# Half of the first mixture's source tiles moved into attention's tail, and VectorE's small tiles of routing in a PSUM bank of its own

## The chip, the cores and the metric

The kernel runs on one core of one Trainium2 chip. The metric is the device time of one execution in microseconds (us), the median of several. Engines: PE is TensorE, DVE is VectorE, ACT is ScalarE, POOL is GpSimd, SP is the engine that issues the DMAs here.

## The reference

Four layers with a residual each, on x of shape (2, 1024, 128), all in float32. The change touches the first two and the routing of the fourth.

```
x = x + attn_a(layernorm(x))     # 16 heads of 64, keys serve as values, causal, out @ W_out (1024 x 128)
x = x + ffn(layernorm(x))        # mixture of experts, with its own inner residual
x = x + attn_b(layernorm(x))     # gated state-space layer with a convolution of 3 taps
x = x + ffn(layernorm(x))

def ffn(x):
    logits = sigmoid(x @ gate_w + gate_b)                  # 16 experts
    values, idx = top_k(logits, k=2); values /= values.sum()
    y_e = (silu(x @ wg_e) * (x @ wu_e)) @ wd_e             # for each expert, inner width 64
    return x + shared_mlp(x) + sum over the two chosen of values * y_e
```

## The kernel before

The 2048 tokens are 16 tiles of 128, or 4 groups of 512 (four tiles each: `PER` is 4, `GROUPS` is 4). x lies in SBUF as `k.x`. The program is a sequence of blocks; inside a block each engine has its own instruction list, and a block's border is passed by all engines together, when the last has finished. Attention is a block, the first mixture (`m1`) the next, then the state-space layer, then the second mixture (`m2`).

**Attention** works in 16 units, each a pair of heads for one of the two batches; unit 14 and 15 are the last pair. A unit's products with the keys, `outputs(g, r)`, come in five bursts, one unit behind the scores. Burst 0 makes the first half of the queries, bursts 1 to 4 the second, in the same PSUM bank `out_ps`, so burst 1 waits until `scale_out(g, 0)` on DVE has read it. POOL adds up the exponentials in `sums`, which lies in the room of `k.x` (its first half of query columns is groups 0 and 2 of x, its second half groups 1 and 3). `denominators(g, half)` (L694 for the last unit) sum these over partitions, ACT inverts them. The scores use three pairs of PSUM banks in turn (`ring_uses`). In the loop's last round, with unit 16, only `outputs(15, r)` and the second denominators are left on TensorE. SP loads W_out (`load_w_out`) at the end of its list.

**A mixture** goes over 36 steps (nine per group: two experts each, the ninth the shared one). A step on TensorE is six matmuls into `g` and `u` and the `down` matmuls of two steps before; ACT makes silu of g, POOL multiplies it with the expert's weight per token (`m_prod`, L1134; the weights come by a DMA into `wb`), DVE multiplies by u (`m_hid`, L1043). The matmuls into `u` wait for hid of two steps before. Everything else is a piece with a time of its own, counted in steps of the group: `agenda` sorts the pieces by `PREPARE`, `OWN`, `FINISH` and `SOURCE_TILES`, and each engine issues its own pieces in that order between the steps. Pieces with a time under 0 come ahead of step 0; of pieces with equal time the order is that of `ORDER`. The pieces are:

- source: eight matmuls per tile of attention's output with W_out (L1715), into the banks of g and u; DVE adds the result to x (L1051)
- statistics, root (ACT, a Sqrt with its own table), norm (DVE: reciprocal L801, then four instructions in `scale_rows`, L96), turn (four transposes, L823), high and low: the split of the normed x into two parts
- residual (POOL, L1143), logits (L963 to L965), sigmoid, natural (transposes back), route1 to route3 (top 2, indices, shares, w: L1077 to L1098), turn_w and w_high; SP then stores w (L1176) and spreads it into wb (L1154)
- add_up and, in m1, the norm for the next layer (`after`), in the finish of a group

In m1 SP first issues the four loads of x, then the eight weight transfers (L1161 to L1169), then the state-space weights (`ahead_of.load`), and only then does its list come to w. ACT waits for all eight transfers ahead of gate_hi (L1005), wg_hi and wu_hi; DVE makes gate_lo (L1070) behind gate_hi, and the logits of group 0 wait for it (`low_split`). `scale_taps` on POOL comes ahead of the residual of group 3, `split_high` and `split_low` of the state-space weights behind the root and the norm of the finish of group 1. A `GroupNorm` named `first` already serves m2: there group 0's source, statistics and root lie in the state-space block.

Of the kernel before, what the change touches and what calls it, by code (L numbers as in the profile page):

```python
# [20 lines left out]
ALU = mybir.AluOpType  # L21
# [78 lines left out]
def layernorm_transposed(nc, s, k, load, banks, xn, sync_first, vector_first, gpsimd_work):  # L100
# [36 lines left out]
    with nc.Block() as block:  # L137
        @block.sync
        def _(sp):
            load(sp, x_loaded)  # L140
            sync_first(sp)
# [82 lines left out]
def ring_uses():  # L224
# [12 lines left out]
    return uses  # L237


def attention(nc, k, w_qk, load_x, load_w_out):  # L240
# [3 lines left out]
    with Scope(nc, "at") as s:  # L244
# [32 lines left out]
        den_ready, ln_done, inv_done, out_used = s.sem("den_ready"), s.sem("ln_done"), s.sem("inv_done"), s.sem("out_used")  # L277
        inv_spread = [s.sem(f"inv_spread{h}") for h in range(2)]
# [90 lines left out]
        with nc.Block() as block:  # L369
            @block.sync  # L370
            def _(sp):
# [21 lines left out]
                load_w_out(sp)  # L393

# [120 lines left out]
            def _(dve):  # L515
# [75 lines left out]
                for half in range(2):  # L591
                    scale_out(UNITS - 1, half)

            @block.tensor
            def _(pe):
# [105 lines left out]

                project(0, "K")
# [48 lines left out]
               low=-12, logits=-10, sigmoid=-9, natural=-8, route1=-8, route2=-8, route3=-7, turn_w=-5, w_high=-5)  # L751
# [8 lines left out]
OWN = {0: dict(norm=-16, residual=-15, turn=-14, high=-13, low=-13, route2=-7, route3=-6),  # L760
# [24 lines left out]
class GroupNorm:  # L785


    def __init__(self, s, tag):
        self.xn = s.sb(f"{tag}_xn", [P, PER, D])
        self.stats, self.moments = s.sb(f"{tag}_stats", [P, PER, 6]), s.sb(f"{tag}_moments", [P, PER, 2])  # L790
        self.sd, self.rstd = [s.sb(f"{tag}_{n}", [P, PER]) for n in ("sd", "rstd")]
        self.small, self.varied, self.rooted, self.normed, self.turned, self.high, self.low = [
# [6 lines left out]
    def norm(self, dve, n, x):  # L799
        dve.wait_ge(self.rooted, n + 1)  # L800
        dve.reciprocal(self.rstd[:, :], self.sd[:, :]).then_inc(self.small, 1)  # L801
# [25 lines left out]
def mixture(nc, tag, k, f, source, source_ready=None, load_x=None, weights=None, next_norm=False, store=None, ahead_of=None, first=None):  # L827
# [9 lines left out]
    with Scope(nc, tag) as s:  # L837
# [10 lines left out]
        x_loaded = [s.sem(f"x_loaded{n}") for n in range(GROUPS if load_x else 0)]  # L848
        sourced, added, summed = s.sem("sourced"), s.sem("added"), s.sem("summed")
        before, after = first or GroupNorm(s, "before"), GroupNorm(s, "after") if next_norm else None  # L850
        early = 1 if first else 0
# [5 lines left out]
        at_f, share = s.sb("at_f", [P, 2, PER]), s.sb("share", [P, 2, PER])  # L857
        picked, parts = s.sb("picked", [P, 2, PER, EXPERTS]), s.sb("parts", [P, 2, PER, EXPERTS])
        den, rec = s.sb("den", [P, PER]), s.sb("rec", [P, PER])
# [17 lines left out]
        def interleave(pieces, emit, step, tiles=False):  # L877

            todo = [item for item in agenda(pieces, next_norm, tiles)
                    if item[2] >= early or item[1] not in ("source", "statistics", "root")]  # L880
# [11 lines left out]
        with nc.Block() as block:  # L892
            @block.tensor
            def _(pe):
# [44 lines left out]
                def emit(piece, n, kind):  # L939
                    if piece == "source":  # L940
                        if source_ready and n == 0 and kind == 0:
                            source_ready(pe)
# [40 lines left out]
            def _(act):  # L983
# [7 lines left out]
                def emit(piece, n, kind):  # L991
                    norm = before if kind == "prepare" else after
                    if piece == "root":
                        norm.root(act, n, k.eps)
                        if ahead_of and n == 1 and norm is after:
                            ahead_of.split_high(act)
# [18 lines left out]
                    elif piece == "w_high":  # L1015
                        act.wait_ge(wt_ready, n + 1)
                        wait(act, wt_stored, 16 * n)
                        act.activation(f.wt[:, :], misc[1][0:EXPERTS, :], ACT.Copy).then_inc(wt_done, 1)
                interleave(("root", "high", "sigmoid", "w_high"), emit, step)

            @block.vector
            def _(dve):
# [22 lines left out]
                def emit(piece, n, kind):  # L1045
                    norm = before if kind == "prepare" else after
                    if piece == "source":
                        dve.wait_ge(sourced, n + 1 - early)
                        if load_x:
                            dve.wait_ge(x_loaded[n], 16)  # L1050
# [3 lines left out]
                    elif piece == "statistics":  # L1054
                        if norm is before:
                            dve.wait_ge(added, n + 1 - early)
# [3 lines left out]
                    elif piece == "norm":  # L1060
# [3 lines left out]
                        if ahead_of and n == 1 and norm is after:  # L1064
                            ahead_of.split_low(dve)
# [684 lines left out]
```

## Time and profile before

| what | value |
|---|---|
| median of 3 runs | 784.04 us (783.72 to 785.32) |
| the profiled execution | 783.28 us |
| its span | 781.5 us |
| PE busy | 729.7 us (93%) |
| DVE / ACT / POOL busy | 458.5 / 375.6 / 424.4 us |
| mean granted clock of TensorE | 0.989 |
| m1's block opens | 492.3 us |
| first step of m1 | 523.44 us |

A busy PE is not a PE at its peak, but an idle PE does nothing: the table and the stretches say where it waits. Idle time of another engine counts only where PE waits for it.

### The profile page before, as it was taken

How to read it: one execution, taken by the hardware profiler on the slowest of the kernel's cores; microseconds unless marked ns; L12 is line 12 of the kernel's file. 1: busy time of each engine (PE TensorE's matmuls, PEld its weight loads, DVE VectorE, ACT ScalarE, POOL GpSimd, SP SyncE). 2: the span in 40 equal slices, each digit the busy share in tenths (PEclk: the TensorE clock that was granted, in tenths of full speed). 3: DMA queues.
4: the chain of work that ended last, by engine and by line, in shares of the span. 5: the costliest groups of instructions: out<-in, count | busy, mean ns of one | idle time of the engine just before them, and what ended most of it. 6: DMA issues, size and time to landing. Idle time of an engine off the chain costs nothing. (4 is left out here: it accounts for less than half of the span.)

```text
span 781.5 us, 14916 instructions
## 1 busy us (share of the span) xinstructions
PE 729.7 (93%) x5653; PEld 495.2 (63%) x5653; DVE 458.5 (59%) x1216; ACT 375.6 (48%) x476; POOL 424.4 (54%) x311
## 2 busy tenths in 40 slices
PE   2779999999999999999999998999989999789998
PEld 1456556555655655655655554887878875668887
DVE  5766665675676675576567540257565547766542
ACT  2355546545555545554654544235644534565421
POOL 4346865775684685676677567015455331344443
PEclk9699999999999999999999999999999999999999
DMA  2000010010010100101001001733222000033222
GB/s 67 7 7 20 19 32 16 22 28 15 22 28 16 25 23 22 25 18 29 15 15 28 16 23 33 177 81 97 76 89 95 29 1 0 3 118 108 91 95 81
DMA packets 41275, 33.47 MB, mean 43 GB/s; under 512 B 14002, under 2 KB 32756, under 8 KB 41204
## 3 DMA queue, kind: packets, MB, share of 16 engines
q1 hardware_dynamic: 41204, 32.52, 14.5%
q8 instruction: 45, 0.74, 0.4%
q14 instruction: 26, 0.21, 0.1%
HBM read 23.32 MB, written 1.31 MB: 32 GB/s over the span
## 5 line engine op out<-in xcount | busy, mean ns | idle before, releaser
L407 POOL TENSOR_TENSOR all_x<-all_x,at_probs 128x1024 f32<-128x1024 f32 (+3 forms) x128 | 215.3, 1682 | 31.8 <-ACT at_probs L487 17.1
L487 ACT ACTIVATE at_probs<-at_ring 128x1024 f32<-128x1024 f32 x144 | 147.5, 1026 | 123.0 <-PE at_ring L662 115.9
L532 DVE CUSTOM_DVE_ANT_0 at_ring<-at_ring,at_after_query 128x128 f32<-128x128 f32 (+3 forms) x256 | 119.5, 520 | 66.3 <-PE at_ring L627 66.3
L680 PE MATMUL at_out<-at_probs,at_k_nat 128*64 128x512 f32 (+3 forms) x768 | 140.3, 494 | 1.1 <-DVE a_attn_t L558 0.9
L407 POOL TENSOR_TENSOR all_x<-at_probs 128x768 f32<-128x768 f32 (+1 forms) x32 | 66.9, 2092 | 126.6 <-ACT at_probs L487 126.4
L1134 POOL TENSOR_TENSOR m_prod<-m_gate,m_wb 128x512 f32<-128x512 f32 x64 | 82.9, 1304 | 96.0 <-ACT m_gate L989 86.1
L680 PEld LDWEIGHTS at_out<-at_probs,at_k_nat 128*64 128x64 f32 x768 | 49.2, 136 | 70.0 <-issue 66.1
L528 DVE TENSOR_REDUCE at_half_max<-at_ring 128x2 f32<-128x1024 f32 x64 | 75.4, 1221 | 11.8 <-PE at_ring L627 11.8
L1043 DVE TENSOR_TENSOR m_hid<-m_prod,m_u 128x512 f32<-128x512 f32 x64 | 43.3, 685 | 66.5 <-POOL m_prod L1134 66.3
L653 PE MATMUL at_ring<-at_qh,at_kh 64*128 64x512 f32 (+3 forms) x384 | 73.8, 380 | 6.1 <-DVE at_m_rows L546 2.6
L909 PEld LDWEIGHTS m_acc<-rest_wd,m_hid 128*128 128x128 f32 x576 | 74.7, 191 | 6.0
L662 PE MATMUL at_ring<-at_m_rows,at_ones_r 64*128 64x512 f32 (+3 forms) x384 | 76.3, 391 | 0.0
L909 PE MATMUL m_acc<-rest_wd,m_hid 128*128 128x128 f32 x576 | 75.2, 275 | 0.0
L989 ACT ACTIVATE m_gate<-m_g 128x512 f32<-128x512 f32 x72 | 42.6, 598 | 66.2 <-PE m_g L901 65.0
L627 PE MATMUL at_ring<-at_kh,at_qh 64*128 64x512 f32 (+3 forms) x384 | 66.0, 393 | 8.4 <-DVE at_half_max L532 2.3
L657 PE MATMUL at_ring<-at_qh,at_kl 64*128 64x512 f32 (+3 forms) x384 | 67.0, 343 | 0.0
L655 PE MATMUL at_ring<-at_ql,at_kh 64*128 64x512 f32 (+3 forms) x384 | 66.9, 343 | 0.0
L653 PEld LDWEIGHTS at_ring<-at_qh,at_kh 64*128 64x128 f32 x384 | 36.6, 187 | 40.9 <-issue 25.6
L627 PEld LDWEIGHTS at_ring<-at_kh,at_qh 64*128 64x128 f32 x384 | 36.4, 190 | 29.4 <-issue 25.5
L519 DVE TENSOR_TENSOR at_ql<-at_ring,at_qh 128x1024 fp32r<-128x1024 f32 x16 | 19.6, 1225 | 51.6 <-ACT at_qh L458 51.6
L558 DVE TENSOR_TENSOR a_attn_t<-at_out,at_inv 128x512 f32<-128x512 f32 x32 | 21.8, 682 | 29.9 <-PE at_out L680 29.9
L657 PEld LDWEIGHTS at_ring<-at_qh,at_kl 64*128 64x128 f32 x384 | 36.5, 186 | 4.4
(244 smaller groups left out, 1256.6 us busy)
## 6 DMA issues: line engine op xcount, KB each, us to landing
m_wb<-m_wt_far SPq DMA_DIRECT2D x128, 128.0 KB, 2.9
at_inv<-at_inv_q SPq DMA_DIRECT2D x240, 32.0 KB, 1.8
all_x<-in_L_attn_a_x SPq DMA_DIRECT2D x8, 256.0 KB, 3.7
at_w_raw<-in_L_attn_a_W_qk SPq DMA_DIRECT2D x8, 128.0 KB, 2.8
out<-all_x SPq DMA_DIRECT2D x4, 256.0 KB, 3.9
a_room<-in_L_attn_a_W_out SPq DMA_DIRECT2D x1, 512.0 KB, 4.1
m_raw_wg<-in_L_ffn_experts_wg SPq DMA_DIRECT2D x1, 512.0 KB, 4.2
m_raw_wu<-in_L_ffn_experts_wu SPq DMA_DIRECT2D x1, 512.0 KB, 4.1
```

Of the source, the lines that this page charges most:

```text
L407: return pool.tensor_tensor(sums[:, :, a * P:b * P], left, right, ALU.add)
L487: act.activation(probs[:, :, slot * BANK:(slot + 1) * BANK], pair("S", unit, slot)[:, :, :], ACT.Exp, scale=BETA).then_inc(exp_done, 1)
L528: last = dve.reduce_max(half_max[:, :, i, out], pair("M", unit, m)[:, :, at:at + w], AX.X)
L532: last = dve.tensor_tensor_reduce(out=sums_ps, in0=sums_ps, in1=after_query[:, BANK - w:BANK], scale=1.0, scalar=MASKED, op0=ALU.add, op1= ...
L627: last = pe.matmul(out[:, l, at:at + (b - a) * P], qh[u][rows(l), i * P:(i + 1) * P], kh[u][rows(l), a * P:b * P], start=True, stop=True)
L653: pe.matmul(to[l], kh[u][rows(l), keys], qh[u][rows(l), q], start=True, stop=False)
L655: pe.matmul(to[l], kh[u][rows(l), keys], ql[u][rows(l), q], start=False, stop=False)
L657: pe.matmul(to[l], kl[u][rows(l), keys], qh[u][rows(l), q], start=False, stop=False)
L662: last = pe.matmul(to[l], ones_r[rows(l), :], m_rows[u][rows(l), q], start=False, stop=True)
L680: last = pe.matmul(out_ps[rows(l), o:o + (b - a) * P], k_nat[g % 3][:, j, rows(l)], probs[:, l, at:at + (b - a) * P], start=(j == 0), stop ...
L909: last = pe.matmul(acc[:, t * P:(t + 1) * P], hid[g % BUFS][:, t * P:(t + 1) * P], f.wd[:, st, :], start=(st == 0 and t == 0), stop=(st == ...
L1134: pool.tensor_tensor(prod[g % BUFS][:, :], gate[g % BUFS][:, :], wb[q % SPREAD][:, :], ALU.mult)\
```

## The change

Attention gets `early`: after bursts 0 and 1 of the last unit TensorE makes two output tiles each (group 0), and after the last burst four more (group 1), into the ring's next pair of banks. SP reloads x in attention's block, groups 0 and 2 once the first denominators of the last unit are made, 1 and 3 after the second. DVE adds the tiles to x there, and makes the statistics of group 0. In m1 the sources 0 and 1 and group 0's statistics are gone from the agenda; its root stays (`rooted=False`). The bank `own` in PSUM holds the inverse deviations and routing's rec, at_f, share and parts; the norm becomes `scalar_tensor_tensor` with the deviation as a broadcast operand from PSUM, the two additions of routing become `reduce_sum`. route2 moves by one step for groups 1 to 3. `scale_taps` goes behind the residual of group 0, `split_high` behind w_high of group 0, and `split_low` to POOL behind the residual of group 1.

```diff
+                for half in range(2):                      # sync, end of attention
+                    sp.wait_ge(den_ready, dens(UNITS - 1, half + 1))
+                    for n in (half, half + 2):
+                        load_x(sp, n, x_again[n])
...
-                for half in range(2):                      # vector, end of attention
-                    scale_out(UNITS - 1, half)
+                def add_early(n):
+                    dve.wait_ge(sourced, n + 1)
+                    dve.wait_ge(x_again[n], 16)
+                    x = k.x[:, n * PER:(n + 1) * PER, :]
+                    dve.tensor_tensor(x, x, pair("X", UNITS)[:, n, :].rearrange("p (t d) -> p t d", t=PER), ALU.add)\
+                       .then_inc(added, 1)
+                scale_out(UNITS - 1, 0)
+                add_early(0)
+                dve.wait_ge(added, 1)
+                first.statistics(dve, 0, k.x[:, 0:PER, :])
+                scale_out(UNITS - 1, 1)
+                add_early(1)
...
+                def early_tiles(a, b):                     # tensor
+                    if a == 0:
+                        early_ready(pe)
+                        pe.wait_ge(out_used, 2 * (UNITS - 1))
+                        pair_free(pe, "X", UNITS)
+                    for t in range(a, b):
+                        last = early(pe, t, pair("X", UNITS)[:, t // PER, t % PER * P:(t % PER + 1) * P])
+                        if t % PER == PER - 1:
+                            last.then_inc(sourced, 1)
...
                         if unit:
                             outputs(unit - 1, r)
+                        if unit == UNITS and r < 2:
+                            early_tiles(2 * r, 2 * r + 2)
                         if r == 1 and unit:
                             denominators(unit - 1, 1)
...
+                early_tiles(PER, 2 * PER)                  # behind the last burst
...
-               low=-12, logits=-10, sigmoid=-9, natural=-8, route1=-8, route2=-8, route3=-7, turn_w=-5, w_high=-5)
+               low=-12, logits=-10, sigmoid=-9, natural=-8, route1=-8, route2=-7, route3=-7, turn_w=-5, w_high=-5)
-OWN = {0: dict(norm=-16, residual=-15, turn=-14, high=-13, low=-13, route2=-7, route3=-6),
+OWN = {0: dict(norm=-16, residual=-15, turn=-14, high=-13, low=-13, route3=-6),
...
-        scale_rows(dve, self.xn, x, self.moments, self.rstd, self.normed)
+        for t in range(PER):                               # where the norm has a bank
+            last = dve.scalar_tensor_tensor(out=self.xn[:, t, :], in0=x[:, t, :], scalar=self.moments[:, t, 0:1],
+                                            in1=self.bank[:, t:t + 1].to_broadcast([P, D]), op0=ALU.subtract, op1=ALU.mult)
...
+        own = s.ps("own")                                  # rstd, rec, at_f, share, parts are slices of it
...
-                        dve.tensor_tensor(den[:, :], top[:, :, 0], top[:, :, 1], ALU.add)
+                        dve.reduce_sum(den[:, :], top[:, :, 0:2], AX.X)
-                        dve.tensor_tensor(w[:, :, :], parts[:, 0, :, :], parts[:, 1, :, :], ALU.add).then_inc(w_ready, 1)
+                        dve.reduce_sum(w[:, :, :], parts.rearrange("p r t e -> p t e r"), AX.X).then_inc(w_ready, 1)
...
                     pool.tensor_tensor(grp(k.xr, n), grp(k.x, n), before.xn[:, :, :], ALU.add).then_inc(summed, 1)
+                    if ahead_of and n == 0:
+                        ahead_of.scale_taps(pool)
+                    if ahead_of and n == 1:
+                        ahead_of.split_low(pool)
...
-                    if load_x:                             # sync, start of the mixture
-                        load_x(sp, x_loaded)
```

## Rows read from the trace of the kernel before

**Rows 1.** Windows: stretch, its us, busy us by engine, granted clock, DMA share, GB/s

```profile
481.70:492.30 10.60, 6.90 (x38) 2.41 (x37) 1.38 (x2) 1.24 (x3) 3.76 (x4) 1.00 0.00 0
...
492.30:508.80 16.50, 16.48 (x147) 16.50 (x148) 5.45 (x21) 5.65 (x7) 1.86 (x5) 1.00 0.86 211
```

**Rows 2.** Waits of TensorE (total, times, longest), 527 to 617, then 684 to 781.5

```profile
PE m_u L899 <- DVE m_hid L1043: 4.3, 5, 1.5
...
PE m_u L899 <- DVE m_hid L1043: 2.8, 4, 1.2
```

**Rows 3.** Timeline of TensorE: start, us, engine, line, operation, [idle before <-releaser]

```profile
482.60 1.51 PE L680 MATMUL at_out<-at_probs,at_k_nat 128*64 128x512 f32 x8 [0.89 <-DVE a_attn_t L558]
...
485.78 1.08 PE L694 MATMUL at_misc<-all_x,at_ones 128*64 128x512 f32 x4 [1.67 <-POOL all_x L407]
...
486.69 4.47 PE L680 MATMUL at_out<-at_probs,at_k_nat 128*64 128x512 f32 x24
...
492.32 12.74 PE L1715 MATMUL m_g<-a_room,a_attn_t 128*128 128x128 f32 x112 [1.16 <-PEq L369]
...
504.90 0.60 PE L823 MATMUL m_misc<-all_ident,m_before_xn 128*128 128x128 f32 x4
...
508.83 0.47 PE L963 MATMUL m_misc<-all_xhi,rest_gate_hi 128*16 128x512 f32 x1
```

**Rows 4.** Timeline of SP's queue, then DMA issues with KB and us to landing

```profile
492.28 2.02 SPq L1678 DMA_DIRECT2D all_x<-in_L_attn_a_x  x4
...
495.86 0.42 SPq L1164 DMA_DIRECT2D m_raw_wg<-in_L_ffn_experts_wg  x1
...
501.39 0.85 SPq L1169 DMA_DIRECT2D rest_wd<-in_L_ffn_shared_wd  x1
...
m_raw_wg<-in_L_ffn_experts_wg SPq DMA_DIRECT2D x1, 512.0 KB, 4.2
...
rest_wd<-in_L_ffn_shared_wd SPq DMA_DIRECT2D x1, 32.0 KB, 4.1
```

**Rows 5.** Timeline of ACT and VectorE in the first mixture's opening

```profile
492.29 1.28 ACT L813 ACT_TABLE_LOAD   x1 [4.09 <-PEq L369]
...
506.03 0.21 ACT L1005 ACTIVATE rest_gate_hi<-m_gate_raw 128x16 fp32r<-128x16 f32 x1
...
506.77 0.17 DVE L1070 TENSOR_TENSOR rest_gate_lo<-m_gate_raw,rest_gate_hi 128x16 fp32r<-128x16 f32 x1
```

**Rows 6.** Windows with the granted clock behind the busy times; then the page's slices

```profile
38.00:41.70 3.70, 0.80 (x18) 0.58 (x16) 2.24 (x2) 2.41 (x4) 0.00 (x0) 0.95 0.02 4
...
41.80:45.10 3.30, 3.22 (x14) 2.08 (x15) 0.02 (x1) 0.74 (x1) 0.00 (x0) 0.50 0.00 0
...
PEclk9699999999999999999999999999999999999999
```

**Rows 7.** Routing's share: ns min/median/max over eight; then the timeline around one

```profile
L1090 DVE TENSOR_TENSOR m_share<-m_top,m_rec x8: 166/1110/1145, 513.8 to 742.2; 128x8 f32<-128x8 f32 x8
...
718.20 3.91 POOL L1134 TENSOR_TENSOR m_prod<-m_gate,m_wb 128x512 f32<-128x512 f32 x3 [2.23 <-ACT m_gate L989]
...
718.38 1.12 DVE L1090 TENSOR_TENSOR m_share<-m_top,m_rec 128x8 f32<-128x8 f32 x1
...
720.48 0.50 PE L899 MATMUL m_u<-all_xhi,rest_wu_hi 128*128 128x512 f32 x1 [0.72 <-DVE m_hid L1043]
```

**Rows 8.** Timeline where the last group's residual and the taps meet

```profile
566.30 2.34 POOL L1242 TENSOR_TENSOR rest_w_raw<-rest_w_main,rest_tap_row 128x256 f32<-128x256 f32 x3
...
567.20 3.99 DVE L96 TENSOR_SCALAR m_after_xn<-all_x,m_after_moments,m_after_rstd 128x128 f32<-128x128 f32 x4
...
571.89 0.50 PE L899 MATMUL m_u<-all_xhi,rest_wu_hi 128*128 128x512 f32 x1 [1.45 <-DVE m_hid L1043]
```

**Rows 9.** Timeline: w of group 2; TensorE's wait in m2's opening

```profile
561.57 0.23 DVE L1098 TENSOR_TENSOR m_w<-m_parts 128x64 f32<-128x64 f32 x1
...
681.54 0.60 PE L978 MATMUL m_misc<-all_ident,m_w 128*16 128x128 f32 x4 [1.74 <-DVE m_w L1098]
```

More of the change, by code:

```diff
@@ L139, in _ @@
         def _(sp):
-            load(sp, x_loaded)
+            for n in range(GROUPS):
+                load(sp, n, x_loaded[n])
             sync_first(sp)
@@ L236, in ring_uses, with attention @@
                 uses.append(("K", unit + 2, 0))
[L237 to L240 removed]
+    return uses + [("X", UNITS, 0)]
+def attention(nc, k, w_qk, load_x, load_w_out, early, early_ready, first):
     uses = ring_uses()
@@ L824, in turn, with mixture @@
         last.then_inc(self.turned, 1)
-def mixture(nc, tag, k, f, source, source_ready=None, load_x=None, weights=None, next_norm=False, store=None, ahead_of=None, first=None):
+def mixture(nc, tag, k, f, source, first, early=1, rooted=True, weights=None, next_norm=False, store=None, ahead_of=None):
     with Scope(nc, tag) as s:
@@ L847, in mixture @@
         hid_ready, down_done, acc_used, stored = s.sem("hid_ready"), s.sem("down_done"), s.sem("acc_used"), s.sem("stored")
-        x_loaded = [s.sem(f"x_loaded{n}") for n in range(GROUPS if load_x else 0)]
         sourced, added, summed = s.sem("sourced"), s.sem("added"), s.sem("summed")
-        before, after = first or GroupNorm(s, "before"), GroupNorm(s, "after") if next_norm else None
-        early = 1 if first else 0
+        before, after = first, GroupNorm(s, "after") if next_norm else None
+        own = s.ps("own")
+        before.bank = own[:, 0:PER]
+        if next_norm:
+            after.bank = own[:, PER:2 * PER]
+        at = 2 * PER
+        rec, at = own[:, at:at + PER], at + PER
+        at_f, at = own[:, at:at + 2 * PER].rearrange("p (r t) -> p r t", r=2), at + 2 * PER
+        share, at = own[:, at:at + 2 * PER].rearrange("p (r t) -> p r t", r=2), at + 2 * PER
+        parts = own[:, P:P + 2 * PER * EXPERTS].rearrange("p (r t e) -> p r t e", r=2, t=PER)
         score_t = s.sb("score_t", [EXPERTS, BANK])
@@ L877, in interleave, with done @@
         def interleave(pieces, emit, step, tiles=False):
-            todo = [item for item in agenda(pieces, next_norm, tiles)
-                    if item[2] >= early or item[1] not in ("source", "statistics", "root")]
+            def done(piece, n, kind):
+                if kind == "finish":
+                    return False
+                return piece == "source" and n < early or n == 0 and (piece == "statistics" or piece == "root" and rooted)
+            todo = [item for item in agenda(pieces, next_norm, tiles) if not done(*item[1:])]
             for g in range(-1, NSTEPS):
@@ L1709, in rest @@
     with Scope(nc, "m1w"):
-        w_out = k.room[:, :].rearrange("r (p n) -> r p n", p=PAIRS)
-        def attention_out(pe, tile, out):
-            for p in range(PAIRS):
-                last = pe.matmul(out, k.attn_t[:, p * TOKENS + tile * P:p * TOKENS + (tile + 1) * P], w_out[:, p, :],
-                                 start=(p == 0), stop=(p == PAIRS - 1))
-            return last
-        mixture(nc, "m1", k, f, attention_out, source_ready=lambda pe: pe.wait_ge(w_out_loaded, 16), load_x=load_x,
-                weights=pick("ffn_"), next_norm=True, ahead_of=ssm)
+        mixture(nc, "m1", k, f, attention_out, k.first, early=2, rooted=False, weights=pick("ffn_"), next_norm=True,
+                ahead_of=ssm)
     with Scope(nc, "m2w") as w:
```

57 lines of the change are left out of this document (31 added, 26 removed).

## The prediction

> **What bounds the kernel now.** I read the busy time by stretch first [rows 1], then what TensorE waits for [rows 2], then the order of time around the change. TensorE is full almost everywhere: from 492.3 to 508.8 it is busy 16.48 of 16.50 us, and in the 10.6 us ahead of that only 6.90 [rows 1]. In steady work of both mixtures it waits for hid alone: five waits, 4.3 us, in the first and four, 2.8 us, in the second [rows 2]. So a stretch is worth what it adds to or takes from TensorE's idle time.
>
> The change touches five idle stretches. Three lie at attention's end [rows 3]: 0.89 us before the burst at 482.60, 1.67 before the denominators at 485.78, and 1.16 at the border of the blocks, 491.16 (486.69 + 4.47) to 492.32; their sum 3.72 is rows 1's 3.70. Then hid's waits, and routing's at the second mixture's start [rows 9].
>
> **Attention's tail.** One tile of output matmul is 16 instructions. 112 take 12.74 us, 0.114 each, so a tile is 1.82 and the eight moved ones 14.6 [rows 3]. The work is the same, only elsewhere. New order on TensorE: burst 0 ends at 481.7 as before (0.89 ahead of 482.60); two tiles to 485.4; burst 1 (1.51) to 486.9, scale_out having ended at 482.6; two tiles to 490.5; denominators and the three last bursts as one piece, 5.38 long (485.78 to 491.16), to 495.9; four tiles to 503.2. The sums that were late at 485.78 are not waited for any more, nor is scale_out. The early tiles' own waits are old: W_out was issued during the last unit, out_used of unit 14 and the ring's banks likewise. x's new loads follow the denominators by over 4 us. VectorE's last addition needs 0.14 + 0.69 and the border 0.3 more, as scale_out's did before, so the first mixture opens at 503.2 + 1.16 = 504.4, 12.1 later than the old 492.3. 14.6 of work moved for 12.1: 2.5 us saved, the two waits of 0.89 and 1.67.
>
> **The first mixture's opening.** Here what hid two latencies is gone. Before, TensorE had 12.6 us of tiles ahead of the first transpose at 504.90 and 16.5 ahead of the logits at 508.83 [rows 3]. Now sources 0 and 1 are gone from the agenda, and the first item of TensorE is the transpose of group 0. It needs the root, which stays in this block: ACT's table load 1.28 and root 0.30 [rows 5], then reciprocal and four normalizations, some 1.4 us; the transpose starts at 504.4 + 3.0 = 507.4. Then one tile of group 2, to 509.8. Then the logits, which wait for gate_lo, and that for gate_hi, and that for all eight weight transfers.
>
> SP issues these transfers in the same block as before, behind the border, so they too start 12.1 later. The four x issues ahead of them (2.02 us of the queue, 1 MB) are gone. Before: first weight matrix issued at 495.86 (3.6 after the block's opening, x and the gate's two issues ahead of it), landed 4.2 later, the last one issued at 501.39 and landed 4.1 later, at 505.5, and gate_hi began at 506.03 [rows 4, 5]. Between those landings lie 5.4 us, with the DMA engines 0.86 busy [rows 1, 4]. After: the first matrix is issued 1.5 after the opening, at 505.9, lands at 510.1, the last at 515.5 by the same pace, somewhat sooner if the pace had owed something to x's backlog. Bounds: 514.5 (x's 2 us and 1 us of backlog off), and 516.1 (the old 11.7 us from gate_w's issue to gate_hi kept). I take 515.2, then gate_hi 0.21 and gate_lo 0.17 with their semaphores, 0.5 [rows 5]: logits at 515.7 instead of 508.83. **From there to the first step the order of TensorE is the old one** and was full before, so the whole kernel is 6.9 us later (bounds 6.3 and 8.0). The 2.5 saved are in this: the idle time is 1.2 + 3.0 + 5.9.
>
> Behind it, sigmoid, routing and the second norm follow gate_hi as before with 7 tiles of TensorE work for cover. SP's long list for the state space ends about 524.5, so the weights of the experts reach wb near 532, close to when POOL asks; cost 0, up to 1 if it is late. POOL's new split_low (a tensor of 128x1024) lies ahead of its first product, under the tiles of group 3: 0.
>
> **The clock.** The trace has a fall. In 38.0 to 41.7 TensorE was busy 0.80 us, and in 41.8 to 45.1 the granted clock is 0.50, which is 1.2 GHz, though TensorE is then busy 3.22 of 3.30 [rows 6]. The new opening has 4.2 us of nothing, 2.3 of work and 5.9 of nothing: longer than any pause between 45 us and the end now. I expect a fall, and a stretch of 3.4 us at half level does 1.7 of full work: +1.7, bounds 0 and 3.4 (two such). The Trainium skill (TensorE: Matmul & The Clock Gate, Why this matters for your kernels) warns that an idle gap between bursts of matmuls brings the array back to half rate. By that rule the change pays the fall on top of the wait, 6.9 + 1.7; if it did not hold, 6.9 alone.
>
> **VectorE's own bank.** m_share works on 8 elements, at least 166 ns, and its median is 1110 [rows 7]: at 718.38 it starts while POOL runs a product begun at 718.20, and sits it out. Then hid is at 719.73 and TensorE has idled 0.72 at 720.48. Six of the nine waits of rows 2 have this form. But hid needs that same product, which ends at 719.5: without the block it starts 0.2 sooner, not 1. So 0.2 each, and not all of it stays: route2 for groups 1 to 3 now follows hid, in the first mixture behind the 1.25 us of the after-norm's statistics too. w, at 561.57 just in time for TensorE [rows 9], comes 0.25 later in group 2 and about 0.5 later in group 3: +0.75, against 0.2 gained in group 1. In the second mixture there are no such statistics: 3 x 0.2 = 0.6 gained. The Trainium skill (SBUF — State Buffer, Who interferes with whom) says that VectorE with two SBUF inputs waits for a GpSimd instruction which reads SBUF, and does not with one. The trace agrees, 166 against 1110 ns; by the rule in full the share's 0.94 goes each time, and by the rows only 0.2 reaches TensorE.
>
> The largest wait, 1.45 at 571.89, goes: POOL's three tap products from 566.30 (2.34 us) leave this place, and the norm of 3.99 us, held up by POOL, shrinks to about 1.2 [rows 8]. Hid then is some 2 us sooner: -1.45. Steady sum: -1.45 - 0.2 - 0.6 + 0.75 = -1.5; bounds: -7.1 if all waits of rows 2 went, +0.5 if the taps alone helped and the norm in the bank (no fast form of the scalar operation) took longer.
>
> In the second mixture's opening TensorE waits 1.74 for w [rows 9], with POOL idle, so nothing is freed and six small operations now read or write PSUM: +0.3, bounds 0 and 1.
>
> **Sum**: 6.9 + 1.7 - 1.5 + 0.3 = +7.4 us. The profiled execution took 783.28 (span 781.5, 1.8 around it); the median of the three is 784.04, 0.76 above. On the median: **791.4 us**.
>
> **Rivals.**
> 1. No fall of the clock. For it: half level shows only in the first 50 us [rows 6], and 2.3 us of work split the pause. Then +5.7: 789.7. Own chance 0.2.
> 2. Two stretches at half level, since the tiles after the wait start within one: +9.1, 793.1. Chance 0.12.
> 3. The bank frees much more, five of hid's seven us: 7.4 - 3.6 = +3.8, 787.8. Against it: hid's start is set by the product's end. Chance 0.1.
> 4. The other side: **the weights land before TensorE asks.** Without x ahead of them and with idle DMA engines, the three matrices could come side by side, each in the 4.2 us of the first. Then the logits start at 509.8, the shift is 1.0, no clock falls, and the sum is 1.0 - 1.5 + 0.3: 783.8; with the bank worth 4 it is 781.3. It decides at logits by 510, 5.6 us after the opening; against it stand 1.6 MB in 512 KB pieces that each took over 4 us. Chance 0.08, most of it on the faster side.
> 5. The bank does not do what it says (share still near 1.1): +8.1, 792.1. Chance 0.05; in my range.
>
> The forecast has 0.45. Range 786.5 to 793.6: below are rival 4 and part of 3, above part of 2. What a measurement tells from no change is 0.2%, 1.6 us. Faster 0.07, within 0.03, slower 0.9.
>
> **What would show it.** Right: TensorE full from 479 to 503; the block opening near 504.4; the transpose at 507.4; gate_hi near 515 and an idle stretch of 5 to 6 us ahead of the logits, ended through gate_lo; a clock of 0.5 for some us behind it; share at 0.17; no wait of 1.45; waits of hid of 0.5 in place of 0.7. Wrong: logits before 511, a wb wait of POOL at the first steps that reaches TensorE, or VectorE's norm near 2 us.

## The result and the profile after

| what | before | after |
|---|---|---|
| median of the comparison | 784.68 us | 789.1 us |
| ratio of after to before | | 1.0054, 95% interval 1.0036 to 1.0073 |
| the profiled execution (its span) | 783.28 (781.5) | 789.13 (787.3) |
| mean granted clock | 0.989 | 0.978 |
| m1's block opens | 492.3 | 504.6 |
| first logits | 508.83 | 514.34 |
| first step of m1 | 523.44 | 531.60 |

The changed kernel is 4.2 to 4.4 us slower; the prediction was +7.4 and its range began at 786.5. The two profiled executions lie 5.85 apart. Single executions of the kernel before lie near 784 or near 786, and its median moves between them (783.84 to 785.4 below), so kernels are compared by their ratios to it. Windows of the changed kernel (stretch, its us, busy us by engine, clock, DMA share, GB/s) give the frame:

```profile
479.60:503.40 23.80, 23.80 (x182) 17.97 (x180) 3.32 (x11) 2.25 (x3) 5.94 (x4) 1.00 0.08 23
504.60:514.30 9.70, 4.53 (x20) 4.24 (x20) 2.19 (x8) 3.90 (x6) 1.89 (x5) 0.61 0.83 207
514.30:519.50 5.20, 5.16 (x23) 4.28 (x23) 1.23 (x9) 4.03 (x5) 2.27 (x3) 0.50 0.48 94
```

Attention's tail has no gap left: 23.80 of 23.80, where [rows 1, 3] had waits of 0.89 and 1.67. Behind the border TensorE works 4.53 of 9.70 us, and then a full stretch at half clock, which [rows 1] did not have. TensorE's timeline shows which waits (in brackets: idle before, and what ended it):

```profile
481.90 3.84 PE L1741 MATMUL at_ring<-a_room,a_attn_t 128*128 128x128 f32 x32
485.67 1.51 PE L703 MATMUL at_out<-at_probs,at_k_nat 128*64 128x512 f32 x8
487.11 3.84 PE L1741 MATMUL at_ring<-a_room,a_attn_t 128*128 128x128 f32 x32
...
507.64 1.12 PE L867 MATMUL m_misc<-all_ident,a_first_xn 128*128 128x128 f32 x4 [4.04 <-DVE a_first_xn L846]
508.55 3.62 PE L1741 MATMUL m_u<-a_room,a_attn_t 128*128 128x128 f32 x16
514.34 0.61 PE L1016 MATMUL m_misc<-all_xhi,rest_gate_hi 128*16 128x512 f32 x1 [2.17 <-DVE rest_gate_lo L1119]
...
519.68 4.14 PE L1741 MATMUL m_u<-a_room,a_attn_t 128*128 128x128 f32 x32
...
531.60 0.48 PE L954 MATMUL m_g<-all_xhi,rest_wg_hi 128*128 128x512 f32 x1
```

The transpose takes 1.12 instead of 0.60, and the row of one tile is 3.62 us long instead of 1.95: the clock has fallen to 0.5 (1.2 GHz) in the first wait, at 506.7, and it stays there through the second and up to 520.4. What the logits wait for is in the queue of SP and in ACT's row:

```profile
505.47 0.41 SPq L1213 DMA_DIRECT2D m_raw_wg<-in_L_ffn_experts_wg  x1
...
509.80 0.71 SPq L1218 DMA_DIRECT2D rest_wd<-in_L_ffn_shared_wd  x1
...
513.86 0.22 ACT L1056 ACTIVATE rest_gate_hi<-m_gate_raw 128x16 fp32r<-128x16 f32 x1 [4.47 <-DMA rest_wd<-in_L_ffn_shared_wd]
```

So gate_hi comes 9.25 us after the block's opening (513.86 - 504.61), gate_lo and the logits right behind. In the steady parts of both mixtures (534 to 625 and 689 to 787), the waits of TensorE (total, times, longest; the first three lines are m1's, the last is m2's) and the share's duration (ns min/median/max) are:

```profile
PE m_u L954 <- DVE m_hid L1096: 1.8, 3, 1.0
PE m_g L954 <- DVE all_x L1102: 0.9, 1, 0.9
PE m_misc L1031 <- DVE m_w L1147: 0.5, 1, 0.5
...
PE m_u L954 <- DVE m_hid L1096: 1.8, 3, 1.0
```
```profile
L1139 DVE TENSOR_TENSOR m_own<-m_top,m_own x8: 174/174/176, 521.6 to 749.4; 128x8 f32<-128x8 f32 x8
```

Against 4.3 and 2.8 in [rows 2], and 166/1110/1145 in [rows 7]. Where [rows 8] had POOL's taps, a norm of 3.99 us and a wait of 1.45, there is now

```profile
574.39 1.28 POOL L1190 TENSOR_TENSOR rest_xr<-all_x,a_first_xn 128x512 f32<-128x512 f32 x1
...
575.28 1.12 DVE L846 SCALAR_TENSOR_TENSOR m_after_xn<-all_x,m_after_moments,m_own 128x128 f32<-128x128 f32 x4
```

and no wait of TensorE. The page's slices show a second dip of the clock, in m2's opening, where a tile of 16 takes 3.58 us:

```profile
PEclk9699999999999999999999999879999999999999
```
```profile
687.13 0.60 PE L1031 MATMUL m_misc<-all_ident,m_w 128*16 128x128 f32 x4 [1.79 <-DVE m_w L1147]
687.57 3.58 PE L1774 MATMUL m_u<-rest_w_out,m2w_z 128*128 128x128 f32 x16
```

The account, from the first logits to the end: +5.5 at the logits, +2.65 behind them to step 0 (17.26 us instead of 14.61), -2.67 in m1's steps (95.65 instead of 98.32), +1.73 in the state-space layer and m2's opening, -1.42 in m2's steps. Sum +5.8, the difference of the spans.

### The profile page after: what moved, and what is told of

It is laid out like the page before. It is cut to its first block and busy times, and to the rows that moved or that the text cites. A ratio compares the mean times of both kernels' runs of the same rounds, so it can differ in the third digit from the quotient of the medians.

```text
span 787.3 us, 14918 instructions
## 1 busy us (share of the span) xinstructions
PE 735.8 (93%) x5653; PEld 501.1 (64%) x5653; DVE 438.5 (56%) x1215; ACT 375.6 (48%) x476; POOL 429.4 (55%) x312
## 5 line engine op out<-in xcount | busy, mean ns | idle before, releaser
L419 POOL TENSOR_TENSOR all_x<-all_x,at_probs 128x1024 f32<-128x1024 f32 (+3 forms) x128 | 221.8, 1733 | 31.6 <-ACT at_probs L499 16.9
L1183 POOL TENSOR_TENSOR m_prod<-m_gate,m_wb 128x512 f32<-128x512 f32 x64 | 81.3, 1278 | 96.1 <-ACT m_gate L1042 89.0
L685 PEld LDWEIGHTS at_ring<-at_m_rows,at_ones_r 64*128 64x128 f32 x384 | 36.9, 187 | 2.8
```

What stands on the lines that cost most here:

```text
L419: return pool.tensor_tensor(sums[:, :, a * P:b * P], left, right, ALU.add)
L685: last = pe.matmul(to[l], ones_r[rows(l), :], m_rows[u][rows(l), q], start=False, stop=True)
L1183: pool.tensor_tensor(prod[g % BUFS][:, :], gate[g % BUFS][:, :], wb[q % SPREAD][:, :], ALU.mult)\
```

## Experiments

Each kernel was timed against the kernel before on the same chip; a ratio is to that kernel, with its 95% interval, and a difference in us is worked out from the ratio. The median of the kernel before was 784.3 beside the first four, 785.4 beside the next four and 783.84 beside the last three.

**The two halves of the change, each alone.** First the tail without the bank, route2's place and the taps:

```diff
 changed kernel
-        own = s.ps("own")       # bank off, route2 back to -8,
...
-                        ahead_of.scale_taps(pool)   # taps, split_high, split_low back
```

> The changed kernel with the tail alone: the early tiles stay, while routing's tiles, route2's place, the norm's form, the taps and the splits are as in the kernel before. My theory: the opening of the first mixture costs about 8 us (logits 5.5 us late, 2.6 us of half clock behind them), the steady parts gain nothing, so about +6.5 to +8.5 on the kernel before, 791 to 793, slower than the changed kernel by some 4 us. In its trace: waits of TensorE of about 4 us ahead of the first transpose and 2 to 4 ahead of the logits, hid's waits again at 7 us. Rival A (the tail is worth its 2.5 us and the bank is what costs): 782, faster than before. Rival B (the loss is the clock alone): within 3 us of the kernel before.

Measured: 792.74 us, ratio 1.0106 (1.0091 to 1.012). Behind the opening hid's waits are 6.8 us in eight, near the old 7.1 in nine. TensorE in the opening:

```profile
508.25 1.12 PE L867 MATMUL m_misc<-all_ident,a_first_xn 128*128 128x128 f32 x4 [4.03 <-DVE a_first_xn L96]
509.16 2.82 PE L1733 MATMUL m_u<-a_room,a_attn_t 128*128 128x128 f32 x16
515.80 0.61 PE L1008 MATMUL m_misc<-all_xhi,rest_gate_hi 128*16 128x512 f32 x1 [3.82 <-DVE rest_gate_lo L1113]
```

Here the clock came back between the two waits: it was at 0.5 from 507.6 to 511.0, at 1.0 up to the second wait, and at 0.5 again from 514.1 to 521.3. So each of the two waits had a fall of its own, and the tile between them took 2.82.

Then everything but the tail:

```diff
 kernel before
+        own = s.ps("own")       # the bank, reduce_sum, norm as scalar_tensor_tensor,
...
+    route2=-7                   # route2 behind one more step, the taps and splits moved
```

> The kernel before with the other half of the change: bank in PSUM, route2's place, norm's form, taps, splits; no early tiles. My theory after the first comparison of traces: steady parts gain 2.7 us in the first mixture and 1.4 in the second, the opening is the old one, so 4.1 less than before, about 780.6. By the prediction's own term it would be 1.2 less, 783.5. Rival A (the bank costs): 785 or more. In its trace: share at 170 ns, hid's waits at 3.5 us instead of 7.1, the first step near 523.4.

Measured: 780.13 us, ratio 0.9947 (0.9933 to 0.9962): 4.2 us faster, and better than both kernels. The halves add up: +8.3 and -4.2 make +4.1, and the change is +4.2. So the tail is a loss of 8.3 us and the rest a gain of 4.2, and within the intervals nothing between them has to be explained.

**Clock or wait?** The two idle stretches of the opening are filled with matmuls whose result nobody reads (12 matmuls, 24 instructions, ahead of the transpose; 16, or 32 instructions, ahead of the logits).

```diff
 changed kernel
+                def keep_busy(pe, count):
+                    for _ in range(count):
+                        pe.matmul(misc[1][:, 0:P], k.attn_t[:, 0:P], k.room[:, 0:P], start=True, stop=True)
...
+                            keep_busy(pe, fill[0])           # 12, ahead of group 0's transpose
...
+                            keep_busy(pe, fill[1])           # 16, ahead of group 0's logits
```

> The changed kernel with 12 idle matmuls into an unused bank ahead of group 0's transpose and 16 ahead of group 0's logits, 2.8 and 3.7 us at full clock, so that TensorE works while it waits. Their results are used by nobody. My theory (half clock comes from the two pauses): the logits stay at about 514.3, since gate_lo sets them, the granted clock is 1.00 through the opening, the first step comes 2.6 us sooner, near 529, and the kernel takes 786.5. Rival B (the clock alone is the loss, the waits cost nothing beside it): 781 to 782. Rival C (the fall has other causes): half clock again and 789 or more.

Measured: 787.13 us, ratio 1.0031 (1.002 to 1.0043).

```profile
505.15 2.92 PE L999 MATMUL m_misc<-a_room,a_attn_t 128*128 128x128 f32 x24 [1.05 <-PEq L374]
508.14 0.66 PE L868 MATMUL m_misc<-all_ident,a_first_xn 128*128 128x128 f32 x4
508.64 1.95 PE L1752 MATMUL m_u<-a_room,a_attn_t 128*128 128x128 f32 x16
...
516.11 0.41 PE L1027 MATMUL m_misc<-all_xhi,rest_gate_hi 128*16 128x512 f32 x1 [1.95 <-DVE rest_gate_lo L1130]
...
530.65 0.48 PE L955 MATMUL m_g<-all_xhi,rest_wg_hi 128*128 128x512 f32 x1
```

The clock stays at 1.0 (tile 1.95, transpose 0.66), and from the logits to step 0 it is 14.54 us, not 17.26: the fall costs 2.7 behind the logits. It costs nothing ahead of them, for there TensorE still waits 2.17 at the end. The logits were expected at 514.3 and came at 516.11: the block opened 0.5 later in this profile, and gate_hi came 10.5 us after the opening, 9.25 in that of the changed kernel. So step 0 is only 0.95 sooner here. The ratios give a gain of 1.8 over the changed kernel; whether it falls short of 2.7 for the same cause is not shown. The mean granted clocks of all executions bear the profiles out: 0.985 to 0.991 here, 0.976 to 0.985 in the changed kernel. They also say that half level did not last equally long in each of the latter, so 2.7 is the size in one profile.

**Order of the tiles.** The eight tiles that m1 still has are moved ahead: two before the first transpose and three between it and the logits, where there was one.

```diff
 changed kernel, m1 alone
-[-13.4, -9, -7.9, -7.8], [-4.9, -4.8, -4.7, -4.6]
+[-15.4, -15.3, -13.4, -13.3], [-13.2, -9, -7.9, -7.8]
```

> The changed kernel with the eight remaining source tiles moved ahead in TensorE's order of the first mixture: two ahead of group 0's transpose, three between it and the logits, one before natural and two behind it. Nothing else. My theory (the loss is an order without cover over two latencies of the block's opening): the two waits go nearly to nothing, the clock stays at 1.00, logits still near 514.3; behind them the low parts of the weights and the second norm are next, so the first step is near 524.5 instead of 531.6 and the kernel takes 782, 2.5 less than before. Rival D (the wait only moves behind the logits, since everything else hangs on the same weights): first step 528 or later, 786 to 787. Rival A (the loss is not in this opening): 789.

Measured: 782.82 us, ratio 0.9981 (0.9969 to 0.9993): one list of times turns a loss of 4.2 into a gain of 1.5. It is still 2.7 us behind the kernel without the tail.

```profile
505.26 3.81 PE L1743 MATMUL m_u<-a_room,a_attn_t 128*128 128x128 f32 x32 [1.05 <-PEq L374]
...
516.76 0.40 PE L1018 MATMUL m_misc<-all_xhi,rest_gate_hi 128*16 128x512 f32 x1 [1.89 <-DVE rest_gate_lo L1121]
...
526.58 0.63 PE L869 MATMUL m_misc<-all_ident,a_first_xn 128*128 128x128 f32 x4 [2.62 <-DVE a_first_xn L848]
527.08 0.50 PE L956 MATMUL m_g<-all_xhi,rest_wg_hi 128*128 128x512 f32 x1
```

The idle time is 1.9 and 2.6 in place of 3.0 and 2.2 (4.04 is 3.0 and the border), and no clock falls in this opening. The second transpose is late: it waits for the norm of group 1, which VectorE makes behind w and the low parts of wg and wu (522.56 to 525.18), and four tiles fewer lie behind the logits to hide that. Step 0 at 527.08 is 2.6 later than the theory had it. As long as the logits wait for the last transfer, the 14.6 us of tiles cover what is in front or what is behind, not both.

**What the logits wait for.** The gate's two transfers get a semaphore of their own; wg_hi and wu_hi move behind the first sigmoid and wait for the six others.

```diff
 changed kernel
-                            act.wait_ge(loaded, 16 * 8)
-                            act.wait_ge(padded, 3)
+                            act.wait_ge(gate_loaded, 32)
                             act.activation(f.gate_hi[:, :], gate_raw[:, :], ACT.Copy).then_inc(split, 1)
...
                         if weights and n == 0:               # behind the sigmoid
+                            act.wait_ge(loaded, 16 * 6)
```

> The changed kernel with one more edit: gate_hi waits only for the gate's own two transfers (a semaphore of their own), and wg_hi and wu_hi are made behind the first sigmoid and wait for the six others. If the logits wait for nothing but the eight transfers, they start right behind the one tile that follows the first transpose, at 510.5 to 511.5 instead of 514.34; the idle stretch ahead of them is under 0.5 us, the granted clock stays at 1.0 or has one half stretch of 3.4 us, step 0 comes at 525.5 to 527 instead of 531.6, and the time is 4.5 to 6 us under the changed kernel's, 783 to 784.5. Rival: the matrices' own splits, or the experts' weights in wb behind SP's long list (it ended near 526), are late next; then step 0 or POOL's first product waits: 785 to 787.

Measured: 783.84 us, ratio 0.9977 (0.9966 to 0.9988), which is 7.7 thousandths or 6 us under the changed kernel.

```profile
508.55 0.77 PE L867 MATMUL m_misc<-all_ident,a_first_xn 128*128 128x128 f32 x4 [4.05 <-DVE a_first_xn L846]
509.11 3.51 PE L1744 MATMUL m_u<-a_room,a_attn_t 128*128 128x128 f32 x16
512.38 0.48 PE L1016 MATMUL m_misc<-all_xhi,rest_gate_hi 128*16 128x512 f32 x1
512.69 0.39 PE L1017 MATMUL m_misc<-all_xlo,rest_gate_hi 128*16 128x512 f32 x1
...
515.42 1.17 ACT L1066 ACTIVATE rest_wg_hi<-m_raw_wg 128x1152 fp32r<-128x1152 f32 x1 [1.40 <-DMA rest_wd<-in_L_ffn_shared_wd]
```

The logits wait for nothing, 3 us ahead of the last landing, and the clock comes back to 1.0 with them (0.39 per matmul): half level lasts 3.4 us here. The first wait, of 4.05, is all that is left, and it alone was enough for the fall. The kernel without the tail is still 2.4 us faster (0.9947).

**The bank's half, taken apart.** The bank alone, with route2 and the taps in their old places:

```diff
 kernel before
+        own = s.ps("own")
+        before.bank = own[:, 0:PER]      # and after.bank, rec, at_f, share, parts, both reduce_sum
```

> The kernel before with the bank of VectorE's own alone (inverse deviations, rec, at_f, share, parts, the two sums); route2 keeps its old place and the taps and splits keep theirs. Theory of the prediction: hid behind share needs the product that blocks share, so a wait of 0.7 loses only 0.2: the waits stay at five and four in number, the tap wait shrinks from 1.45 to about 0.3 since the norm of 3.99 becomes 1.12, total -1.5 to -2 us. Rival: share and the other small operations were held by a product that the next hid does not need, so they cost TensorE nearly the whole 0.7 each: share at 0.17, three or four waits gone, total -3.5 to -4.2, that is all that the bank, the order and the taps gave together (4.2).

The taps alone:

```diff
 kernel before
-                    if ahead_of and n + 1 == GROUPS:
-                        ahead_of.scale_taps(pool)
...
+                    if ahead_of and n == 0:              # behind the residual; split_high: behind w_high
+                        ahead_of.scale_taps(pool)
+                    if ahead_of and n == 1:
+                        ahead_of.split_low(pool)
```

> The kernel before with only the state-space weights' work moved: scale_taps behind the first residual, split_high behind the first w_high, split_low to POOL behind the second residual. The wait of 1.45 near 571.9 should go or shrink to at most 0.7, all others stay: -0.8 to -1.5 us against before. Rival: the norm on VectorE shares its port with POOL's residual and product anyway and stays near 3.5 to 4 us, the wait of 1.45 stays: 0 to -0.3.

Route2 alone:

```diff
 kernel before
-route2=-8     # PREPARE; OWN loses its route2=-7
+route2=-7
```

> The kernel before with only route2 one step later in groups 1 to 3, behind that step's hid. By the prediction it costs: w is late by 0.5 to 0.75 us, hid's waits move one step, total 0 to +0.8. Rival: route2, held by POOL's product for 1.1 us, was what stood ahead of a hid whose own product had long been made; behind it, the hid is on time and the waits of 0.7 go: -1 to -2.5 us.

Measured: bank 783.46 us, ratio 0.9981 (0.9969 to 0.9993); taps 783.92, 0.9991 (0.998 to 1.0001); route2 785.72, 1.0004 (0.9994 to 1.0015). In us: -1.5, -0.7 and +0.3, together -1.9, while the three in one kernel give -4.2. The intervals are wide for this (about 0.8 to 1.2 us each way for each of the four), so by the times alone the difference of 2.3 is only just clear, and the taps and route2 alone are not told from no change. The waits in the profiles show it directly: the three need each other. Those of TensorE from 524 to the end, hid's and w's, of the bank alone, the taps alone, route2 alone, and all three:

```profile
PE m_u L913 <- DVE m_hid L1057: 5.8, 9, 1.5
PE m_misc L992 <- DVE m_w L1112: 1.8, 1, 1.8
```
```profile
PE m_u L899 <- DVE m_hid L1043: 6.4, 9, 1.2
PE m_misc L978 <- DVE m_w L1096: 1.9, 2, 1.7
```
```profile
PE m_misc L978 <- DVE m_w L1098: 5.4, 6, 1.7
PE m_u L899 <- DVE m_hid L1043: 5.1, 7, 1.4
```
```profile
PE m_u L913 <- DVE m_hid L1057: 3.6, 6, 1.0
PE m_misc L992 <- DVE m_w L1110: 2.3, 2, 1.8
```

Before it was 7.1 and 1.9. So the waits move by -1.4, -0.7, +1.5 (together -0.6) and -3.1; the times follow within 0.1 for the first two, and are 1.2 and 1.1 better than the waits for the others. A part of that is seen: a matmul that has waited takes 0.50, another 0.40, so a wait costs 0.1 beyond itself. The rest is open. Two mechanisms make the three more than their sum. The wait of 1.45 has two causes in a row, POOL's taps (which make its next product late) and the norm of 3.99 on VectorE: in the kernel with the bank alone the norm is 1.12 and TensorE still waits 1.45 at 572.18, where 0.3 was expected; with the taps alone the norm is 3.31 and it waits 0.70 at 572.18; with both it waits not at all. And route2 behind hid frees hid, but as long as its small operations are held by POOL it makes w late: six waits for w, 5.4 us. In the bank they are short, and w loses 0.3 in one group. That the bank alone gave the expected -1.5 was luck: the wait of 1.45 stayed, and instead the waits of group 3 went, the 0.70 in m2 whole, while in m1 one of 0.36 stands in place of the 0.72.

**Repairs.** The small state-space loads are issued three at a time between the later spreads, so that SP's list doesn't stand ahead of the store of w:

```diff
 kernel with the gate's semaphore
-        sp.wait_ge(self.loaded, self.count)
...
                             spread(n, st)
+                            if ahead_of:
+                                ahead_of.drip(3)
+                    if ahead_of:
+                        sp.wait_ge(ahead_of.loaded, ahead_of.count)
```

> The kernel with the gate's own semaphore, and in addition SP issues the small state-space loads three at a time between the later spreads of the weights, and waits for them at the end of its list, not ahead of the first store of w. In the kernel with the gate's semaphore alone the first spread was issued at 529.19 and the second hid wait was 1.88 long, behind POOL's product of 533.16 that waited for wb. If SP's list is what held it, the store of w is issued near 520.5, the product follows ACT's gate at once, the 1.88 goes, and the time is 1.5 to 2.2 under that kernel's: 781.6 to 782.4. Rival: the loads that are dripped in hold back the spreads, and POOL waits for wb in later steps: no gain or a loss, 784 or more.

Measured: 782.59 us, ratio 0.998 (0.9971 to 0.9989); the kernel with the gate's semaphore alone had 0.9977. In its profile w is stored at 519.25, not 527.59, and the longest of m1's waits for hid is 1.0 and not 1.9, as expected; the medians show no gain. The profiled execution of the kernel with the semaphore alone, 784.86, was 1 us above its own median, so that wait is likely not in all of them.

Group 3's addition ahead of the second low part, on the kernel without the tail:

```diff
-SOURCE_ADDED = [-22, -12.5, -5.5, -1.3]
+SOURCE_ADDED = [-22, -12.5, -5.5, -4.2]
```

> The kernel with everything of the change but the tail (bank, route2's place, taps), and the addition of group 3's source moved from step -1.3 to -4.2 in both mixtures, ahead of the second group's low part. TensorE waits 0.89 for it in m_g of step 1 in each mixture. If the addition lies in the cover of the tiles and nothing needs VectorE more, both waits go: 1.8 under the 780.1 of the kernel without this edit, 778.3. Rival: the low part of group 1, 0.7 later, delays the second logits, and the wait comes back there: 779.5 to 780.5.

Measured: 781.12 us, ratio 0.9964 (0.995 to 0.9977), against 0.9947 (0.9933 to 0.9962) without this edit: no gain. The two waits of 0.9 for all_x are gone, and TensorE waits instead 2.1 for the scores, which was 0.3:

```profile
PE m_misc L986 <- ACT m_score_t L1025: 2.1, 3, 0.9
```

ACT loads a table ahead of a score (550.36, 1.28 us, for group 2). The rows tell no more than that this wait lay hidden behind the other.

All repairs on the changed kernel (the gate's semaphore, the late loads, group 3's early addition), and the root of group 0 in attention's block, one tile ahead of the first transpose and one more ahead of the logits:

```diff
+                first.root(act, 0, k.eps)                        # end of attention's ACT program
+                act.preload_act_table_set("sigmoid_and_others")
...
+AHEAD = SOURCE_TILES[:2] + [[-15.4, -13.4, -9, -7.9], [-7.8, -4.9, -4.8, -4.7]]
```

> All repairs together on the changed kernel: gate's semaphore, late small loads, the addition of group 3 early, the root of group 0 in attention's block (so the first transpose comes 1.5 after the block's opening, not 3.0), one tile ahead of that transpose and one more tile ahead of the logits than in the kernel before this one. Expected: the first transpose waits for nothing, logits near 511.5, no stretch at half clock in the opening, step 0 near 523.5, so that the 2.5 of the tail stay: 775.5 to 777.5, under the kernel that leaves the tail out (778.3). Rival: the second group's norm, behind the splits of wg and wu that wait for the transfers landing near 515.3, sets the second transpose near 524.5 to 525.5, so that the gain of the tail is eaten again: 778 to 779.5.

Measured: 777.66 us, ratio 0.9924 (0.991 to 0.9938), the best of all.

```profile
504.07 2.02 PE L1754 MATMUL m_u<-a_room,a_attn_t 128*128 128x128 f32 x16 [1.05 <-PEq L374]
505.93 0.60 PE L870 MATMUL m_misc<-all_ident,a_first_xn 128*128 128x128 f32 x4
...
508.08 0.48 PE L1019 MATMUL m_misc<-all_xhi,rest_gate_hi 128*16 128x512 f32 x1
...
520.55 0.60 PE L870 MATMUL m_misc<-all_ident,a_first_xn 128*128 128x128 f32 x4
520.91 0.48 PE L957 MATMUL m_g<-all_xhi,rest_wg_hi 128*128 128x512 f32 x1
```

No wait but the border's 1.05 in the whole opening, the clock at 1.0, step 0 at 520.91: 2.5 us ahead of the old 523.44, of which 0.3 lies ahead of the tail in this profile (burst 0 begins at 479.02 for 479.34). That is about the tail's gain (0.89 + 1.67) as the prediction had it, once nothing takes it back. The second transpose waits for nothing; VectorE's split of wg began at 515.22, as expected, and ended soon enough. No run leaves the tail out of this last kernel, so what the tail is worth in time is bounded only by its neighbours: 1.8 us under the kernel without the tail, 3.1 under that kernel with group 3's early addition.

## Why the prediction was right, and where its terms were off

**The tail: right.** Two waits gone, the block open at 504.61 for 504.4. In the last kernel step 0 is 2.5 us sooner than before, and its time is 1.8 us under that of the kernel without the tail (0.9924 against 0.9947); the two intervals overlap a little, and that kernel has other repairs too.

**The root: right.** 507.64 for 507.4.

**The weights: right in kind, 1.4 too late in this profile.** The logits waited for gate_lo and gate_hi and these for the transfer issued last; taking only that condition away starts them with no wait. The working had 515.7 and the profile has 514.34. The step that was off is the pace of the transfers: the last was issued 5.2 after the opening, not 6.7, and landed 4.0 later. But this term has a spread of its own: from opening to gate_hi it was 9.25, 10.1, 10.5 and 11.1 us in the profiles of four kernels with the same list (the changed one, the tail alone, filled, tiles first). The predicted 10.8 (515.2 - 504.4) is within these. The bounds of this term are off by 0.1 and 0.2: logits 0.5 behind 514.5 and 516.1 make 6.2 and 7.8, not 6.3 and 8.0.

**The clock: right in kind, too small.** I took one stretch that does 1.7 less work. The clock was at half level from 506.7 to 520.4, 13.7 us, and cost 2.65 behind the logits. The second wait has a part in this: without it (the gate's semaphore) half level lasted 3.4 us, and with the tail alone it began anew in it. The filled kernel shows that it is the idle stretches which do this. The Trainium skill (TensorE: Matmul & The Clock Gate, Why this matters for your kernels) warns of idle gaps between bursts of matmuls; the trace agrees, with a fall to 0.5 inside the wait of 4.04. The sum of the two steps, 8.6 at step 0, came out as 8.16 because one error went against the other.

**The bank: the term that was mis-sized.** The working gave -1.5 in the steps and +0.3 in m2's opening; measured are -4.1 (-2.67 and -1.42, the opening's own wait 1.79 for 1.74), and -4.2 in the kernel without the tail. The 1.45 went as said. What failed is "hid needs that same product": the rule was read off one row, 718.20, which is group 2, and taken for all. There it holds: 0.72 became 0.55, and 1.20 became 1.03 in group 1, 0.2 each. In group 3 it does not. Timeline of the kernel before, m2's group 3:

```profile
738.45 2.53 POOL L1134 TENSOR_TENSOR m_prod<-m_gate,m_wb 128x512 f32<-128x512 f32 x2 [2.63 <-ACT m_gate L989]
...
741.94 1.28 POOL L1134 TENSOR_TENSOR m_prod<-m_gate,m_wb 128x512 f32<-128x512 f32 x1 [0.96 <-DMA m_wb<-m_wt_far]
...
742.15 1.09 DVE L1090 TENSOR_TENSOR m_share<-m_top,m_rec 128x8 f32<-128x8 f32 x1
...
744.22 0.50 PE L899 MATMUL m_u<-all_xhi,rest_wu_hi 128*128 128x512 f32 x1 [0.70 <-DVE m_hid L1043]
```

Here the product that the next hid needs ended at 741.0, and the share was held by the one after it: hid had its product for over 2 us, and the whole 0.70 of TensorE's wait at 744.22 was route2's. The kernel with the bank alone, where route2 keeps its place, doesn't have this wait. That makes -0.70 in m2 and -0.72 in m1, where I had 0.2 and nothing. Another part of the error is w: I had +0.75 for its delay, and it was +0.33, in one group. Group 3 (0.72 and 0.50), group 2 of m1 (0.19, not counted), w (0.42), three waits fewer at 0.1 each and m2's opening (0.25) are 2.4 of the 2.8 us by which -4.04 is beyond -1.2; the rest is open. The Trainium skill (SBUF — State Buffer, Who interferes with whom) agrees in its rule, 174 ns in place of 1110; what this is worth was the schedule's to say.

**m2's opening: +0.05 for +0.3**, so the operands in PSUM cost next to nothing here. The dip of the clock behind it, 1.7 us, I don't put down to the change: its wait, 1.79, is the old 1.74, and the kernel with the taps alone, which has no tail and no bank, had the same dip in its profile, while the kernels with the bank alone and the filled one had none. What causes it is open. Without it the profiled difference is 4.1, which is what the medians give.

**What was costed at nothing stayed there**: the spread of w began at 527.60 and POOL's first product had its gate as releaser; split_low on POOL, 2.35 us at 527.81, ended ahead of it. One reading left something out: TensorE waits in the steady work not for hid alone, but also 0.9 for all_x in each mixture and 0.2 for w. The 0.9 are the same in both kernels.

So the forecast (slower, by the waits in the opening and a fall of the clock) was right; the profiled +5.85 is the working's +7.4 less 2.8 for the bank and 0.45 for the opening, plus 1.7 for the dip in m2. Rival 3 (the bank frees much more) was largely true beside it. The time itself, 789.1, lies nearer to rival 1's 789.7 and rival 3's 787.8 than to the forecast's 791.4. The clock did fall, so it is the rows and not the time that tell the forecast from rival 1.

## What to carry to other kernels

Work that is taken from in front of a latency is not only moved: ask which two or three things it hid, and bring them forward with it. Here the tail brought the first step 2.5 us forward only when the root, the gate's small transfers (their own semaphore) and the order of two tiles went with it: +4.2 became -6, with two smaller repairs among them that showed no gain by themselves. And when a stall's worth is read from one instance, read the others too: whether the held instruction is late depends on which product the one behind it needs, and that changed from group to group.

## What the runs showed of the hardware

- An idle stretch of 4 us in m1's opening took the clock to 0.5. With a second wait of 2.2 us behind it half level lasted from 506.7 to 520.4; without the second wait it lasted 3.4 us; in the kernel with the tail alone it ended between the waits and began again in the second, of 3.8 us. With the same waits filled by matmuls the clock stayed at 1.0.
- A wait of 1.8 us in m2's opening was followed by a stretch at half level in four of the 13 profiles (the changed kernel, tiles first, the taps alone, the addition early) and not in the others. What decides it is open.
- The same eight transfers, in the same order and with an idle queue ahead, were in use 9.25 to 11.1 us after their block opened.
- VectorE's operation on 8 elements of each partition took 1110 ns (median) with its operands in SBUF, beside a POOL product, and 174 with one of them in PSUM. Four norms of 128 elements took 3.99 or 3.31 us as tensor_scalar beside POOL, and 1.12 beside POOL with the deviation in PSUM; where POOL did nothing, tensor_scalar took 1.12 as well.
